# Two fused transformer layers: layer 1's feed-forward in steps beside its attention, layer 0's experts packed into fewer rounds

## The chip, the cores and the metric

The kernel runs on one core of one Trainium2 chip. The metric is the device time of one execution, in microseconds. The kernel before takes 2185.24 us (median of 3 runs, 2185.12 to 2186.42).

## The reference, cut to what matters

```
x: (8, 512, 256), so 4096 tokens of 256 numbers, all float32
xn = layernorm(x)
x  = x + attention0(xn) + experts(xn)           # layer 0
xn = layernorm(x)
x  = x + attention1(xn) + feed_forward(xn)      # layer 1

attention0:   16 heads of 16, softmax(q k') v, no mask, no output projection
experts:      8 experts; each token goes to the one with the largest x @ centroids';
              layernorm, relu(h w1' + b1) w2' + b2, 256 -> 1024 -> 256,
              mixed in with alpha = sigmoid(affinity)
attention1:   causal attention, then a convolution of width 3 over its output makes new
              queries, then a second causal attention with the same k and v, then out_w
feed_forward: P = x @ U1 (256 -> 64);  H = gelu(P @ V1 + b1) (64 -> 1024, tanh form);
              (H @ U2) (1024 -> 64) @ V2 (64 -> 256) + b2
```

## The kernel before, in words

The 4096 tokens are 32 tiles of 128 rows, 4 tiles to each of 8 batch items b. The sum x stays in SBUF (tile X, float32) through both layers. Each engine (PE, DVE, ACT, POOL, SP) runs one object whose `program` method walks the same lists of steps and issues only what belongs to that engine. So the order on every engine is written out by hand, by generators ("lanes") that are merged: `weave` spreads the steps of each lane evenly over one round, `interleave` takes one step of every lane in turn, or every second or third.

Attention is cut into units: one batch item and 8 of the 16 heads. Layer 0 has 16 units (numbers 0 to 15). Layer 1 has 32 (16 to 47): 16 of the first causal attention (kind 1), 16 of the second (kind 2), in the order 1.0, 1.1, 2.0, 1.2, 2.1, and so on, two units each. In the round of unit i run: `expp` of unit i (scores transposed on PE, L825, with a mask product L829 if causal; exp on ACT, L1625; the product with v on PE, L842), `maxp` of unit i+1 (scores on PE, L804; row maxima on DVE, L1199 or, causal, L1193; they are split into three bfloat16 rows and sent by DMA), and the projection of unit i+2 (`pre0`, `pre1`). A projection to q and k goes PE, L765 or the convolution L1017; ACT, L1603 (high part); DVE, L1151 (rest); POOL, L1839 and L1841 (middle and low part); then 6 DMAs from SP (`fan`), after which `maxp` may start.

Layer 0's expert feed-forward is a lane beside rounds 1 to 14: 39 tiles of up to 128 tokens of one expert, in two passes over halves of the hidden width, since only half the weights fit in SBUF. Pass `first` runs in rounds 1 to 7, 34 steps a round; in round 8 the weights of the second half are loaded (16 DMAs of 512 KB from ACT's queue, L1588 and L1590) and no expert step runs; pass `second` runs in rounds 9 to 14. Each tile's result goes to a DRAM buffer `ysd`.

Then comes `ffn`, a stage of its own between the layers: POOL gathers each token's row from `ysd` (L1911), DVE adds it to X with alpha (L1431) and computes the layer norm (L1071, L1139, with the square root's iteration on POOL, L1784 to L1790); PE transposes (L724, method `near`) and multiplies by U1 (L948); method `far` multiplies by V1 in 3 bfloat16 products (L965) into one of 3 PSUM banks, ACT computes the gelu (L1711, one instruction on 128x512), PE multiplies by U2 (L979), and `tail` by V2 (L992), which DVE adds to X (L1492). POOL adds the biases to X (L1944). All 8 items pass through this, about two at a time. The last items have the projections of units 16 and 17 beside them. ACT loads another function table before the first gelu and the exp table again after the last.

In layer 1 the maxima rotate over three PSUM banks, the projections and transposes share one bank (Ma), and the transposes of the attention's output have another (Mb). `fin1` transposes the second attention's output (L724, L1751) and multiplies it by out_w (L1043).

## Time and profile before

| | |
|---|---|
| median of 3 runs | 2185.24 us |
| profiled execution, its own time | 2184.84 us |
| its span, first to last instruction | 2183.0 us |
| PE busy | 1844.7 us, 85% |
| DVE busy | 1256.3 us, 58% |
| ACT busy | 1019.4 us, 47% |
| POOL busy | 363.4 us, 17% |
| mean granted TensorE clock | 0.934 of full |

A round begins with the first exp of its unit. By these starts, layer 0's unit 1 begins at 208.9 us, unit 2 at 284.1, unit 8 at 607.7, unit 9 at 650.0, unit 14 at 942.3, unit 15 at 986.6 (its attention ends at 1011); unit 16, the first of layer 1, begins at 1225.0. From 1345.4 on the rounds repeat in periods of four units (two of kind 2, two of kind 1). The table and the rows below are to be read with these borders. A PE that is busy in the profile may still have gaps between short matmuls, since the ends of matmuls are modelled.

### The profile page before, as it was taken

To read this page: it belongs to the slowest core of one execution; us is meant where nothing else is said; L and a number is where in the kernel's file an instruction comes from. 1 tells how busy PE (TensorE), PEld (TensorE's weight loads), DVE (VectorE), ACT (ScalarE), POOL (GpSimd) and SP (SyncE) were. 2 spreads that over 40 slices of the span, in tenths; PEclk is the share of its full clock that TensorE was granted. 3 is DMA by queue.
4 is the path that set the end of the run, shared out by engine and by line. 5 is a ranking of instruction groups with operands and counts; after the bars stand their busy time and mean duration, and the time that the engine had idled before them with its cause. 6 is when DMAs were issued, how large, how long until landed. Compare 5 with 4: busy or idle time off the path is not lost.

```text
span 2183.0 us, 31789 instructions
## 1 busy us (share of the span) xinstructions
PE 1844.7 (85%) x10767; PEld 904.5 (41%) x10777; DVE 1256.3 (58%) x3777; ACT 1019.4 (47%) x2048; POOL 363.4 (17%) x555
## 2 busy tenths in 40 slices
PE   3575799999979999994689788989898989989877
PEld 2341355554424444541234343444444444444434
DVE  4554455555554454553552775667575757666653
ACT  0232455655645555563354254445454545444444
POOL 2215211111101121213442100010010101000000
PEclk8557899999999999997799899999999999999999
DMA  7245343334374444413104245255553535452550
GB/s 144 68 141 140 67 83 71 80 72 81 64 203 57 71 62 71 61 28 92 32 20 73 38 57 74 41 75 68 69 74 56 74 53 67 65 78 41 66 59 21
DMA packets 145968, 155.87 MB, mean 71 GB/s; under 512 B 26008, under 2 KB 132784, under 8 KB 145808
## 3 DMA queue, kind: packets, MB, share of 16 engines
q1 hardware_dynamic: 123872, 114.75, 34.0%
q0 software_dynamic: 10048, 14.44, 3.7%
q10 hardware_dynamic: 11888, 24.64, 3.5%
q8 instruction: 88, 1.44, 0.3%
q14 instruction: 72, 0.59, 0.1%
HBM read 55.95 MB, written 33.72 MB: 41 GB/s over the span
## 4 chain that ended last, share of the span: by engine, by line
PE 60%; DVE 15%; DMA 6%; issue 6%; ACT 5%; POOL 4%; SPq 4%; DVEq 0%; ACTq 0%; POOLq 0%
PE p_PV L842 11%; PE p_S L804 8%; PE p_S L825 7%; DVE p_S L1193 5%; PE p_Ma L1017 4%; PE p_Ma L765 4%; SPq L1981 4%; PE p_Mb L896 4%; PE p_S L919 4%; DMA t_R<-ks 3%; PE p_Ma L773 2%; DVE t_rr L1151 2%; ACT t_spl L1603 2%; ACT t_R L1625 2%; POOL idd L1873 1%
## 5 line engine op out<-in xcount | busy, mean ns | idle before, releaser
L1625 ACT ACTIVATE t_R<-p_S 128x512 f32<-128x512 f32 (+1 forms) x1216 | 669.2, 576 | 469.4 <-PE p_S L829 312.1
L1193 DVE CUSTOM_DVE_ANT_0 p_S<-p_S,t_NM 128x128 f32<-128x128 f32 (+3 forms) x1024 | 473.1, 522 | 141.7 <-PE p_S L804 138.8
L804 PE MATMUL p_S<-t_R 96*128 96x512 bf16 (+3 forms) x1536 | 454.8, 338 | 67.0 <-DMA t_R<-ks 34.2
L1199 DVE TENSOR_REDUCE t_mx<-p_S 128x1 f32<-128x512 f32 x512 | 346.2, 686 | 255.2 <-PE p_S L804 242.5
L825 PE MATMUL p_S<-t_R 99*128 99x512 bf16 (+3 forms) x1536 | 466.6, 331 | 16.8 <-ACT t_R L1625 6.5
L842 PE MATMUL p_PV<-t_R 128*17 128x512 f32 (+3 forms) x3072 | 324.1, 494 | 8.9 <-ACT t_R L1625 8.7
L804 PEld LDWEIGHTS p_S<-t_R 96*128 96x128 bf16 x1536 | 135.5, 99 | 393.3 <-issue 167.2
L1839 POOL CAST t_spl<-t_rr 128x512 bf16<-128x512 f32 x80 | 49.0, 612 | 996.7 <-DVE t_rr L1151 996.7
L825 PEld LDWEIGHTS p_S<-t_R 99*128 99x128 bf16 x1536 | 150.2, 98 | 150.8 <-ACT t_R L1625 73.2
L829 PE MATMUL p_S<-t_NM 128*128 128x128 bf16 x1024 | 195.6, 220 | 0.0
L1193 DVE DVE_READ_ACCUMULATOR2_ANT t_mx<- 128x1 f32 x1024 | 144.9, 141 | 0.0
L829 PEld LDWEIGHTS p_S<-t_NM 128*128 128x128 bf16 x1024 | 101.0, 99 | 39.3 <-issue 8.3
L896 PE MATMUL p_Mb<-t_R,t_NM 128*128 x184 | 97.0, 608 | 7.6 <-DMA t_NM<-hTd 3.1
L919 PE MATMUL p_S<-t_R,t_NM 128*128 x392 | 100.9, 379 | 0.0
L842 PEld LDWEIGHTS p_PV<-t_R 128*17 128x17 f32 x3072 | 50.9, 95 | 115.9 <-issue 87.1
L1017 PE MATMUL p_Ma<-t_NM,t_R 128*128 128x512 f32 x192 | 97.8, 664 | 0.0
L1841 POOL TENSOR_TENSOR t_spl<-t_rr,t_spl 128x512 bf16<-128x512 f32 x80 | 92.6, 1157 | 6.4
L1151 DVE SCALAR_TENSOR_TENSOR t_rr<-p_Ma,t_BQK,t_spl 128x512 f32<-128x512 f32 x48 | 36.0, 751 | 97.2 <-ACT t_spl L1603 97.2
L919 PEld LDWEIGHTS p_S<-t_R,t_NM 128*128 128x128 f32 x392 | 73.7, 190 | 17.9 <-issue 2.3
L1603 ACT ACTIVATE t_spl<-p_Ma,t_BQK 128x512 bf16<-128x512 f32 x48 | 33.0, 688 | 91.1 <-PE p_Ma L765 81.6
L1603 ACT ACTIVATE t_spl<-p_Ma,t_CB 128x512 bf16<-128x512 f32 x16 | 11.0, 687 | 131.1 <-PE p_Ma L1017 131.1
L765 PE MATMUL p_Ma<-t_R,t_WQ 128*128 128x512 f32 x128 | 63.9, 623 | 7.2 <-DVE t_rr L1151 5.8
(236 smaller groups left out, 2114.1 us busy)
## 6 DMA issues: line engine op xcount, KB each, us to landing
t_R<-t_spl SPq DMA_DIRECT2D x480, 128.0 KB
t_R<-in_w ACTq DMA_DIRECT2D x32, 512.0 KB, 8.8
t_R<-ks SPq DMA_DIRECT2D x96, 128.0 KB
ks<-t_spl SPq DMA_DIRECT2D x16, 384.0 KB, 7.4
...
```

The lines of the kernel that those rows point to most:

```text
L765: t = self.nc.tensor.matmul(M[:, :], m.WQ[:, cc, off:off + 128], xT[:, cc, :], start=(cc == 0), stop=(cc == 1))
L804: t = self.nc.tensor.matmul(bank[:, z, :], qa[0:96, h, qb * 128:(qb + 1) * 128], ka[0:96, h, 0:n], start=True, stop=True)
L825: t = self.nc.tensor.matmul(bank[:, z, :], ka[0:99, h, kb * 128:(kb + 1) * 128], qa[0:99, h, n0:512], start=True, stop=not u.causal)
L829: t = self.nc.tensor.matmul(bank[:, z, 0:128], m.identb, m.maskk, start=False, stop=True)
L842: t = self.nc.tensor.matmul(m.PV[32 * j:32 * j + 17, n0:512], vt[:, kb, 4 * g + j, :], m.P1[kb][j] if u.causal else m.P[p % 2][:, j, :], s ...
L896: z = self.nc.tensor.matmul(m.MB[i][:, :], m.hT[t % 2][:, c, :], m.W1[:, bass.ds(self.regs[t], 1), c, :], start=(c == 0), stop=(c == 1))
L919: x = self.nc.tensor.matmul(M[:, 0:256], m.AT[:, k, :], m.W2[:, bass.ds(self.regs[t], 1), k * 256:k * 256 + 256], start=(k == 0), stop=(p ...
L1017: t = self.nc.tensor.matmul(M[:, :], m.CW[:, i, c * 128:c * 128 + 128], m.cT[:, cc, k:k + 512], start=(i == 0), stop=(i == 5))
L1193: x = nc.vector.tensor_tensor_reduce(out=sc, in0=sc, in1=m.maskq[:, 512 - n:512], scale=1.0, scalar=NEG, op0=ALU.add, op1=ALU.max, accum_o ...
L1199: nc.vector.tensor_reduce(m.mx[:, g, i:i + 1], m.S1[s1_bank(k)][:, :], AX.X, ALU.max).then_inc(s.s1_read, 1)
L1625: nc.scalar.activation(m.P1X[kb][j0 // per] if u.causal else m.P[p % 2][:, j0:j0 + per, :], m.s2_bank(k)[:, 0:per * n].rearrange("p (j n) ...
L1841: g.tensor_tensor(m.spl[:, z, 2, :], m.rr[:, :], m.spl[:, z, 1, :], ALU.subtract).then_inc(s.lo_done, 1)
```

## The change

The `ffn` stage as a stage is gone. Layer 0 and layer 1 are one loop of 48 rounds.

- Experts: `first` takes 40 steps in each of rounds 1 to 5 and its last 35 in round 6. The load of the second half of the weights is in round 6 behind them. `second` takes 24 steps in round 7 behind a pause, 35 in each of rounds 8 to 11 and the rest in round 12. Rounds 13, 14 and 15 have no expert steps.
- Gathers and norms of layer 1 (`arrive(b)`): items 0 and 1 in rounds 13 and 14, the others in every fourth round from 18. The add of the gathered row and the normalisation move from DVE to POOL (L1718, L1720, L1732); DVE keeps the statistics. Layer 1's weights are requested by SP at round 14, the rest at round 17. Unit 16's and 17's projections are in rounds 14 and 15.
- The feed-forward of item b (`forward(b)`), 19 steps, is spread over four rounds of layer 1 each (item 0 over rounds 15 to 17): U1, split, eight times `wide` and `bend`, then `narrow` (U2 for all eight blocks at once, from a buffer G of 8 x 512 numbers a partition).
- gelu(h) is no longer one ACT instruction. `wide`: ACT adds the bias into G (L1529) and squares into W with the scale sqrt(0.044715) (L1533); POOL adds 1 (L1749) and multiplies by h (L1751). `bend`: ACT tanh (L1547); POOL adds 1 (L1756) and multiplies by h (L1758). The factor 0.5 is applied where `narrow`'s result is copied (L1556). There is one buffer W, so one block is under way at a time.
- V2's product is accumulated into the same PSUM bank as out_w's, in `final(b)`, and DVE adds both to X in one instruction for each half.
- The maxima rotate over two PSUM banks in both layers; every other use in both layers rotates over three (Ma, Mb, S1[2]).
- The second attention's convolution, and with it its k from DRAM, comes earlier in its round: after the third of the 9 steps of its lane (`pre`), where it came at the 13th turn of a lane that ran every second turn. SP issues the loads of q and k in one step.

```diff
-    for i in range(16):
+    forward = [e.forward(b) for b in range(NB)]
+    for i in range(48):
+        b, r = (i - 10) // 4, (i - 10) % 4
+        if i == 14:
+            e.load_layer1()
+        if i == 17:
+            e.load_late()
         lanes = [e.expp(u[i])]
-        if i < 15:
+        if i < 47:
             lanes.append(e.maxp(u[i + 1]))
-        if i < 14:
-            lanes.append(e.pre0(u[i + 2]))
+        if i == 14:
+            lanes.append(chain(e.near(0), steps(1), e.pre(u[16])))
+        elif i == 15:
+            lanes.append(chain(e.pre(u[17]), take(forward[0], 2), e.near(1)))
+        elif i < 46:
+            lanes.append(e.pre(u[i + 2]))
...
-        if 1 <= i < 8:
-            lanes.append(take(first, 34 if i < 7 else 60))
-        if i == 8:
-            lanes.append(e.weights(1))
-        if 9 <= i < 15:
-            lanes.append(take(second, 34 if i < 14 else 60))
+        if 1 <= i < 6:
+            lanes.append(take(first, 40))
+        if i == 6:
+            lanes.append(chain(take(first, 60), e.weights(1), steps(10)))
+        if i == 7:
+            lanes.append(chain(steps(12), take(second, 24)))
+        if 8 <= i < 13:
+            lanes.append(take(second, 35 if i < 12 else 60))
+        if i == 13:
+            lanes.append(e.arrive(0))
+        if i == 14:
+            lanes += [e.arrive(1), e.causal_masks()]
...
+        if i in (16, 17):
+            lanes.append(take(forward[0], 9 if i == 16 else 20))
...
+        if i >= 18:
+            if r == 0 and b < NB:
+                lanes.append(e.arrive(b))
+            if r == 1 and b < NB:
+                lanes.append(chain(steps(2), e.near(b), steps(4)))
+            if i < 46:
+                lanes.append(take(forward[(i - 14) // 4], 5 if (i - 14) % 4 < 3 else 20))
+        if i and u[i - 1].kind == 2 and u[i - 1].c:
+            lanes.append(chain(steps(6), e.final(u[i - 1].b), steps(2)))
         weave(e, *lanes)
```

On ACT:

```diff
+    def wide(self, b, f, i):
+
+        e, m, s, k = self.e, self.m, self.s, 8 * b + f
+        e.wait_ge(s.h_mm, k + 1)
+        e.wait_ge(s.q_mm, b)
+        self.nc.scalar.activation(m.G[:, f, :], m.MB[i][:, :], ACT.Identity,
+                                  bias=m.FBI[:, f:f + 1]).then_inc(s.h_done, 1)
+        e.wait_ge(s.h_done, k + 1)
+        e.wait_ge(s.h_gelu, k)
+        self.nc.scalar.activation(m.W, m.G[:, f, :], ACT.Square, scale=GELU_A ** 0.5).then_inc(s.h_sq, 1)
...
+    def bend(self, b, f):
+        e, m, s, k = self.e, self.m, self.s, 8 * b + f
+        e.wait_ge(s.h_arg, k + 1)
+        self.nc.scalar.activation(m.W, m.W, ACT.Tanh, scale=GELU_C).then_inc(s.h_tanh, 1)
```

On POOL (`bend` there is the same with h_tanh, and writes G):

```diff
+    def wide(self, b, f, i):
+        e, m, s, k = self.e, self.m, self.s, 8 * b + f
+        if f == 0:
+            self.base1(b)
+        e.wait_ge(s.h_sq, k + 1)
+        a = self.mark(self.nc.gpsimd.tensor_scalar(m.W, m.W, 1.0, None, ALU.add))
+        e.wait_ge(s.g_own, a)
+        self.nc.gpsimd.tensor_tensor(m.W, m.W, m.G[:, f, :], ALU.mult).then_inc(s.h_arg, 1)
```

On PE, `wide` and the wait of `maxp` for its PSUM bank:

```diff
+    def wide(self, b, f, i):
+        e, m, s = self.e, self.m, self.s
+        M = self.mbank(i, s.h_done, 8 * b + f + 1)
...
+        for z, (vv, pp) in enumerate(((m.VA, 0), (m.VA, 1), (m.VB, 2))):
+            t = self.nc.tensor.matmul(M[:, :], vv[:, f * 128:(f + 1) * 128], m.PT[:, pp, :],
+                                      start=(z == 0), stop=(z == 2))
+        t.then_inc(s.h_mm, 1)
...
-                if k >= LAYER1 + 3:
-                    e.wait_ge(s.s1_read, k - 2)
-                elif k >= 2:
-                    e.wait_ge(s.s1_read, min(k - 1, LAYER1))
+                if k >= 2:
+                    e.wait_ge(s.s1_read, k - 1)
```

The order of the instructions shows where these steps land. ACT's queue at the load of the second weights (t_R<-in_w; ACTIVATE t_R<-p_S is an exp). Before, in round 8, the first rows:

```order
L1588 DMA t_R<-in_w 128x2x512
L1625 ACTIVATE t_R<-p_S 128x512
L1590 DMA t_R<-in_w 128x1024
L1603 ACTIVATE t_spl<-p_S,t_BQK 128x512
L1625 ACTIVATE t_R<-p_S 128x512
L1588 DMA t_R<-in_w 128x2x512
```

Of the changed kernel, in round 6, behind the last expert tile's copy (L1609):

```order
L1609 COPY t_NM<-p_Mb 128x256
L1444 DMA t_R<-in_w 128x2x512
L1446 DMA t_R<-in_w 128x1024
L1444 DMA t_R<-in_w 128x2x512
L1446 DMA t_R<-in_w 128x1024
L1478 ACTIVATE t_R<-p_S 128x512
L1444 DMA t_R<-in_w 128x2x512
```

The 16 loads have 8 exps among them where they had 29 exps and 2 other instructions.

PE's queue in a round of kind 1, around the convolution for a unit of kind 2 (MATMUL p_Ma<-t_NM,t_R x6). L810 and L903 are the transposes of the maxima that end the first half of `maxp`. Before:

```order
L810 MATMUL p_S<-t_ident,t_mx 16x128
L825 MATMUL p_S<-t_R 128x128
L829 MATMUL p_S<-t_NM 128x128
...
L842 MATMUL p_PV<-t_R 17x256 x4
L804 MATMUL p_S<-t_R 128x128 x4
L1017 MATMUL p_Ma<-t_NM,t_R 128x512 x6
```

Of the changed kernel (p_S<-t_ident,t_R is a transpose of the first attention's output; t_AF holds U1; p_Mb<-t_ident,t_O is the transpose of the output of the unit before):

```order
L751 MATMUL p_S<-t_ident,t_R 128x128 x4
L918 MATMUL p_S<-t_R 128x512
...
L897 MATMUL p_S<-t_R 128x256 x2
L822 MATMUL p_Ma<-t_R,t_AF 128x512 x2
L897 MATMUL p_S<-t_R 128x256 x2
L950 MATMUL p_Mb<-t_ident,t_O 128x128 x4
...
L918 MATMUL p_S<-t_R 128x512
L922 MATMUL p_S<-t_R,t_B1T 128x128
L806 MATMUL p_Ma<-t_NM,t_R 128x512 x6
```

The convolution stands before the transpose of the first half of the maxima, by 25 rows (L806 at row 3526, L903 at 3551 of PE's queue), where it stood behind it by 11 (L810 at 4420, L1017 at 4431).

ACT's queue in layer 1, where a unit of kind 1 is projected (t_spl<-p_Ma,t_BQK). Before:

```order
L1625 ACTIVATE t_R<-p_S 128x512 x4
L1603 ACTIVATE t_spl<-p_Ma,t_BQK 128x512
L1625 ACTIVATE t_R<-p_S 128x512
L1636 COPY t_O<-p_PV 128x512
L1603 ACTIVATE t_spl<-p_Ma,t_BQK 128x512
L1625 ACTIVATE t_R<-p_S 128x512 x2
L1625 ACTIVATE t_R<-p_S 128x384 x4
```

Of the changed kernel (L1529 is the bias add into G, L1533 the square, L1547 the tanh):

```order
L1464 ACTIVATE t_spl<-p_Ma,t_BQK 128x512
L1478 ACTIVATE t_R<-p_S 128x512
L1529 ACTIVATE t_R<-p_Mb,t_GB 128x512
L1533 ACTIVATE t_R<-t_R 128x512
L1490 COPY t_O<-p_PV 128x512
L1464 ACTIVATE t_spl<-p_S,t_BQK 128x512
L1478 ACTIVATE t_R<-p_S 128x512 x2
L1547 ACTIVATE t_R<-t_R 128x512
L1478 ACTIVATE t_R<-p_S 128x384 x4
L1478 ACTIVATE t_R<-p_S 128x512
L1529 ACTIVATE t_R<-p_S,t_GB 128x512
L1533 ACTIVATE t_R<-t_R 128x512
```

Between square and tanh, and between tanh and the next square, stand 2 to 6 other instructions. ACT's queue has one ACT_TABLE_LOAD in the changed kernel, at its start, and three before.

## Rows read from the trace of the kernel before

**Rows 1.** The page: busy time of each engine, then 40 slices.
```profile
PE 1844.7 (85%) x10767; PEld 904.5 (41%) x10777; DVE 1256.3 (58%) x3777; ACT 1019.4 (47%) x2048; POOL 363.4 (17%) x555
PE   3575799999979999994689788989898989989877
```

**Rows 2.** Busy by stretch: from:to, length, each engine (count), clock, DMA share, GB/s.
```profile
208.90:284.10 75.20, 51.91 (x240) 26.32 (x241) 32.69 (x64) 30.65 (x69) 24.00 (x26) 0.82 0.28 55
284.10:607.70 323.60, 316.52 (x1567) 163.09 (x1565) 187.90 (x357) 191.80 (x433) 59.06 (x66) 1.00 0.38 75
607.70:650.00 42.30, 34.24 (x154) 10.32 (x154) 26.48 (x50) 19.61 (x35) 4.98 (x6) 0.92 0.84 223
650.00:942.30 292.30, 279.24 (x1309) 142.71 (x1310) 141.09 (x248) 161.53 (x374) 53.68 (x63) 0.98 0.42 67
942.30:986.60 44.30, 43.59 (x215) 21.15 (x213) 25.08 (x45) 27.99 (x65) 6.03 (x8) 1.00 0.17 25
986.60:1011.00 24.40, 19.05 (x103) 3.53 (x103) 3.35 (x9) 17.38 (x33) 2.12 (x3) 1.00 0.05 7
1011.00:1225.00 214.00, 143.21 (x557) 60.94 (x568) 110.79 (x301) 71.92 (x111) 80.42 (x152) 0.84 0.24 54
1464.80:1584.20 119.40, 106.27 (x790) 52.60 (x786) 80.29 (x314) 56.26 (x107) 10.61 (x12) 0.99 0.49 66
```

**Rows 3.** PE's waits from 1011 to 1225: us in total, times, longest.
```profile
PE p_Ma L724 <- DVE t_NM L1139: 32.6, 3, 22.5
PE p_S L965 <- DVE t_R L1482: 15.7, 5, 5.7
```

**Rows 4.** Timeline of PE at 1120 to 1135: start, us, what.
```profile
1120.57 1.88 PE L948 MATMUL p_Ma<-t_R 128*128 128x512 f32 x4
1124.04 1.47 PE L965 MATMUL p_S<-t_R 128*128 128x512 bf16 x6
1125.44 1.08 PE L979 MATMUL p_S<-t_R 128*64 128x512 f32 x4
1131.79 1.03 PE L992 MATMUL p_Mb<-t_R 128*128 128x256 f32 x4
1132.65 0.60 PE L724 MATMUL p_Ma<-t_ident,t_NM 128*128 128x128 f32 x4
```

**Rows 5.** PE's waits from 607.7 to 655.
```profile
PE p_S L765 <- DMA t_R<-in_w: 4.6, 1, 4.6
PE p_S L765 <- DMA t_xTb<-xTd: 3.4, 1, 3.4
```

**Rows 6.** PE's waits from 1464.8 to 1584.2, one period of layer 1.
```profile
PE p_S L804 <- DMA t_R<-ks: 3.2, 1, 3.2
PE p_Mb L856 <- ACT t_O L1636: 2.3, 5, 0.7
PE p_Ma L724 <- DVE t_rr L1151: 1.6, 1, 1.6
PE p_Ma L773 <- DVE t_rr L1151: 0.9, 2, 0.5
PE p_Ma L765 <- DVE t_rr L1151: 0.8, 2, 0.4
```

**Rows 7.** Groups by line: busy us, mean ns, idle before. First three 1011 to 1225.
```profile
L1711 ACT ACTIVATE t_R<-p_S,t_R 128x512 f32<-128x512 f32 x64 | 43.5, 687 | 50.6 <-PE p_S L965 40.5 <-remote 7.9 <-PE p_PV L979 1.1
L1693 ACT COPY t_R<-p_Ma 128x512 f32<-128x512 f32 x16 | 9.4, 586 | 40.6 <-PE p_Ma L724 40.6
L1625 ACT ACT_TABLE_LOAD x1 | 1.3, 1283 | 6.5 <-POOL t_X L1944 6.5
L1841 POOL TENSOR_TENSOR t_spl<-t_rr,t_spl 128x512 bf16<-128x512 f32 x6 | 6.9, 1158 | 0.5
L1839 POOL CAST t_spl<-t_rr 128x512 bf16<-128x512 f32 x6 | 3.7, 611 | 108.2 <-DVE t_rr L1151 108.2
```

**Rows 8.** Durations of one line: ns min/median/max, first and last start.
```profile
L1841 POOL TENSOR_TENSOR t_spl<-t_rr,t_spl x80: 1149/1157/1162, 31.2 to 2104.2; 128x512 bf16<-128x512 f32 x80
L1856 POOL TENSOR_TENSOR t_X<-t_X,t_on x32: 719/724/1052, 180.9 to 1012.3; 128x256 f32<-128x256 f32 x32
```

More of the change, by code:

```diff
@@ L568, in add_norm, with pre @@
     def add_norm(self, b, k): pass
-    def pre0(self, u):
-        if u.c == 0:
+    def pre(self, u):
+        if u.kind == 2:
+            if u.c == 0:
+                if u.b in (0, NB - 1):
+                    yield from steps(5)
+                for cc in range(2):
+                    self.turn_c(u.b, cc, self.bank())
+                    yield
+            self.convolve(u, self.bank())
+            yield
+            yield from steps(6)
+            return
+        if u.kind == 0 and u.c == 0:
             self.load_x(u.b)
@@ L1620, in scores @@
         elif u.causal:
[L1621 to L1622 removed]
+            e.wait_ge(s.pv_mm, 128 if kb else 127)
         elif p >= 2:
@@ L1704, in far @@
-    def far(self, b):
-        nc, e, m, s = self.nc, self.e, self.m, self.s
-        for f in range(8):
-            k = 8 * b + f
-            e.wait_ge(s.v1_mm, k + 1)
-            if k >= 4:
-                e.wait_ge(s.u2_mm, k - 3)
-            nc.scalar.activation(m.HT[k % 4], m.hb[k % 3][:, :], ACT.Gelu_apprx_tanh,
-                                 bias=m.FBI[:, f:f + 1]).then_inc(s.gelu, 1)
-            yield
-    def tail(self, b):
-        e, m, s = self.e, self.m, self.s
-        e.wait_ge(s.u2_mm, 8 * b + 8)
-        if b >= 2:
-            e.wait_ge(s.y2_mm, 2 * b - 2)
-        self.nc.scalar.copy(m.QS[b % 2], m.qb[b % 2][:, :]).then_inc(s.qs_done, 1)
-        yield from steps(4)
```

966 lines of the change are left out of this document (405 added, 561 removed).

## The prediction

> **What bounds the kernel now.** I read the page first: PE is busy 85% of the span, DVE 58%, ACT 47%, POOL 17% [rows 1]. So PE bounds, and the question is where its 338 idle us lie. I cut the span at the borders of the rounds [rows 2]. In rounds 2 to 7 (expert steps beside attention) PE is busy 316.5 of 323.6 us, in rounds 9 to 13 279.2 of 292.3. Round 8, without expert steps, has 34.2 of 42.3. The stage between the layers takes 214 us, with PE busy 143.2, at a mean clock of 0.84. A period of layer 1 (4 units) takes 119.4 us, with PE busy 106.3, DVE 80.3, ACT 56.3 and POOL 10.6. PE's waits in the stage are a start (32.6 us in 3 waits for normalised rows) and a hand-over from DVE (15.7) [rows 3]. Waits in a period are small and many: k from DRAM 3.2 us, the rest of the split (t_rr) 1.6 + 0.9 + 0.8, the output's copy 2.3 [rows 6].
>
> No matmul goes away. The change takes PE work of a stage that PE fills to two thirds and puts it where PE is filled to 89%. So the gain is the idle time that vanishes, less the waits that the steps bring with them.
>
> **Layer 0, rounds 1 to 15.** PE is busy 51.9 + 316.5 + 34.2 + 279.2 + 43.6 = 725.5 us in rounds 1 to 14 [rows 2]. Rounds 13 and 14 now hold attention only. What such a round takes I read from round 8: 42.3 us, less 3.4 us of waiting for x [rows 5], less about 3.4 us for its half clock. The last is worked out from the mean clock 0.92: 8% of 42.3 us lost against full clock is 3.4 us. That leaves 35.5 us, of which PE works 34.2 - 3.4 = 31. Rounds 1 to 12 keep the rest of the work: 725.5 less 6.8 for the clock of rounds 8 and 9, less 31 for round 13, less 26 for round 14 (it had no projection, about 5) = 662. Their idle time: 23.3 in round 1 (routing, unchanged), 11 rounds at 1.3 = 14 (rounds 2 to 7 show 7.1 for six), and for the weights 3. Sum 702, so round 12 ends at 208.9 + 702 = 911.
>
> On the weights: before, PE waits 4.6 us for them after a whole round of spaced loads [rows 5]. Now the 16 loads stand within a quarter of round 6 (the order: 8 exps among them), some 14 us. 8.4 MB at the 223 GB/s of round 8 [rows 2] take 38 us, at the rate of a quiet moment less. The first expert step that needs them is a third into round 7, about 16 us in. Loads begin some 23 us before round 6 ends, so they have 39 us: just enough. I take 3 us, bounds 0 and 15.
>
> Round 13: 35.5 us. Round 14: 37, with the first transposes. Round 15: it took 24.4 without maxima and projection; now it has both, U1 and two transposes: 40. SP issues 12 loads of layer 1 at the head of round 14, ahead of that round's maxima and its fans of 6; POOL's gathers stand before its split of q and k. For both I add 3 us, bounds 0 and 25 (the longest wait of rows 3 is 22.5). Layer 1 then starts at 911 + 35.5 + 37 + 40 + 3 = 1026, not at 1225.
>
> **Layer 1, a period.** PE's steps for one batch item, from their rows [rows 4]: V1 24 products at 1.47 - 0.17 per 6 (the tail of one overlaps the next) = 5.2; U2 four pairs at about 0.95 = 3.8; U1 1.7; transposes 2 x 0.55 = 1.1; V2 1.7. Sum 13.5 us, and all of it is on the path, since PE is the bound.
>
> What goes: the convolution stands some 25 rows before the middle of the maxima instead of 11 behind, so k and q start about 5 us earlier and the 3.2 us for k go. Three rotating banks replace the one shared bank (Ma), so of 3.3 us of waits for t_rr I drop 2.8. The clock's 1% is 1. Sum 7.0 [rows 6, 2]. Late next behind k is the copy of O (2.3), which stays.
>
> What comes: ACT gets, per block of the gelu, a bias add of 0.69 (as L1711), a square and a tanh of about 0.59 (as L1693) [rows 7], 1.87 us for 0.69: 15.0 us per item, and 3.5 for four copies and a scaled copy. 56.3 + 18.5 = 75 of 130 us: not the bound. But ACT's queue is in order: in `wide` two instructions, 1.28 us, stand before the next exp, and only two banks lie between PE's scores and the exps. PE meanwhile has its own 0.65 us of V1 and the maxima. I take 0.25 us of stall for each of 16 steps = 4. The bounds are 0 and the whole burst, 8 x (1.28 + 0.59) = 15.
>
> POOL per block: two adds and two products on 128x512. The nearest rows are a one-input cast, 611 ns, and a two-input op, 1157 ns [rows 7]: 3.5 us a block, 28 an item; with joins, normalisation, the split and the base add (together about 18, an estimate from L1856, L1839 and L1841) POOL works 57 of 130 us. A step of `forward` comes every 5.4 us or so (5 in a round of 27), and POOL's pair takes 1.8, so the tanh seldom waits. Two banks for the maxima instead of three: DVE needs 0.7 to 0.9 us for a single maximum, PE sends one each 1.1 us on the average; only bursts wait. This was never seen in layer 1; bounds 0 and 2 a period, I take 0. DVE loses two adds of V2 an item and the gathers' adds, and keeps statistics; at 80 of 130 us that costs nothing.
>
> So a period goes from 119.4 by +13.5 - 7.0 + 4.0 = +10.5. Layer 1's eight items: 8 x 10.5 = 84. From 1225.0 to 2183.0 it took 958.0; now 1042. The two table loads (the gelu's, and the exp's again, 1283 ns) go with the stage [rows 7].
>
> **Sum.** 1026 + 1042 = 2068 of span. The profiled execution was 1.84 us longer than its span, and the median of the runs 0.4 above it: 2070 us, 115 less than 2185 (5.3%).
>
> **A rule that speaks against it.** L1841, the nearest to POOL's new products, took 1149 to 1162 ns in all 80 cases, with DVE at work beside it; L1856, with two float32 inputs, took 724 and once 1052 [rows 8]. The Trainium skill (GPSIMD Engine Reference, Specifications) says that POOL shares its SBUF interfaces with VectorE and contends with it when a DVE instruction runs in a two-port mode or has two SBUF inputs. By the 80 cases nothing is added. By the rule, DVE's new neighbours could stretch POOL's pair; it is the second half of the slower rival below. The skill's ScalarE: Activation LUTs (Table sets) lists tanh in the exp set; no run so far shows a tanh. The built order has no table load in layer 1, and the sum goes by that.
>
> **The rivals.**
> *PE is filled.* The new steps slip into the gaps. A period cannot be under 106.3 + 13.5 = 119.8; with 3 idle it is 122.8, +3.4. Layer 1 takes 958 + 8 x 3.4 = 985; rounds 13 to 15 take PE's own 32 each, so it starts at 911 + 96 = 1007: 1992, as a time 1994. For it: rounds 2 to 7 are filled to 98%. Against it: these steps hang on four engines, expert steps on two.
> *ACT's bursts block the exps.* Two thirds of the full burst: +10 instead of +4, and 48 more in all: 2118; with poor banks for the maxima, 2130. For it: two score banks. Against it: ACT is busy less than half of a period [rows 2], so it catches up.
> *The start stays.* Gathers, norms and weights are still chains: the waits of 32.6 [rows 3] come back in rounds 13 to 15, which also run light on PE and at half clock in part: 2105.
> *The relay is on the path (slower).* For each of the 64 blocks ACT must wait twice for POOL in its own queue, at the tanh and at the next square. If POOL's pair (1.8 us) were exposed each time, 128 x 1.8 = 230 us: 2300. It decides from 115 / 128 = 0.9 us of exposure per hand-over. Contention like the one case of 1052 ns against 724 would make the pair 2.6, which 2 exps between do not cover and 5 do. For it: one W, two engines in order, POOL also with gathers and 12 small steps of the square root between a square and its sum. Against it: the spacing of 5.4 us.
> *It does nothing.* If layer 0 were bound by something else than PE, moving experts would not shorten it, but the stage of 214 us goes in any case.
>
> **Chances.** Forecast 57% (own range 2045 to 2100), PE filled 13%, bursts 15%, start stays 9%, relay slower 4% and 2% at no change. Range to hold 8 in 10: 2015 to 2128, which takes in most of the bursts, all of the start, and the upper part of "PE filled". Faster by over 0.2% (what a measurement of this kernel can tell) 93%, within 0.2% 2%, slower 5%.
>
> **What will show it.** The first causal exp at about 1026; rounds 13, 14, 15 at 35 to 40 us; a period near 130 with PE busy about 120; no wait for the second weights over 5 us; k's wait gone from PE's waits in layer 1; ACT about 75 and POOL about 57 us busy a period; L1749 and L1756 about 0.6 us, L1751 and L1758 about 1.16. I am wrong if the period is over 137 or under 125, if layer 1 starts after 1045, or if ACT's waits for POOL at L1547 and L1533 sum to over 30 us.

## The result, and the profile after

The changed kernel takes 2229.76 us (median of 4 runs, 2224.86 to 2234.62) against 2185.62 in the same session. The ratio is 1.0202, 95% interval [1.0179, 1.0224]: 44 us slower, where 115 faster was forecast. The profiled execution's span is 2232.8 us.

Its page answers to [rows 1]:

```profile
PE 1884.2 (84%) x10777; PEld 910.8 (41%) x10777; DVE 1211.5 (54%) x3653; ACT 1096.7 (49%) x2178; POOL 824.9 (37%) x935
...
PE   3573899999799999988778888888888898888877
```

PE's share is what it was (84% against 85%). The weak slices in the middle (the 4 and 6 of [rows 1], the stage) are gone; in their place the 9s of layer 1 have turned into 8s. The work was moved as planned, but PE is idle as large a share of the time as before.

The stretches, to be held against [rows 2] (from:to, length, busy of PE, PEld, DVE, ACT, POOL with counts, clock, DMA share, GB/s). They are round 1; rounds 2 to 6; 7; 8 to 12; 13; 14; 15; and one period of layer 1:

```profile
215.20:290.80 75.60, 61.21 (x276) 31.02 (x277) 33.39 (x65) 33.19 (x75) 17.88 (x20) 0.86 0.29 62
290.80:589.80 299.00, 288.53 (x1390) 150.55 (x1388) 159.74 (x306) 169.42 (x388) 53.08 (x59) 0.98 0.42 96
589.80:648.20 58.40, 49.51 (x227) 22.70 (x228) 28.13 (x51) 30.47 (x69) 8.63 (x10) 0.97 0.44 82
648.20:946.30 298.10, 284.66 (x1323) 145.23 (x1321) 139.96 (x244) 163.51 (x376) 54.38 (x65) 0.98 0.41 63
946.30:988.20 41.90, 33.98 (x157) 9.95 (x158) 29.04 (x61) 19.44 (x36) 26.31 (x43) 0.92 0.36 59
988.20:1033.10 44.90, 38.14 (x165) 11.26 (x164) 30.14 (x61) 20.31 (x38) 22.16 (x40) 0.85 0.60 114
1033.10:1073.20 40.10, 33.04 (x167) 11.20 (x166) 23.71 (x84) 24.95 (x44) 13.00 (x12) 0.91 0.37 50
1376.30:1519.60 143.30, 123.80 (x849) 59.69 (x846) 85.28 (x326) 73.85 (x136) 76.20 (x75) 0.95 0.42 58
```

Round 12 ends at 946.3 (forecast 911). Rounds 13 to 15 take 41.9, 44.9 and 40.1 (forecast 35.5, 37, 40, and 3). Layer 1 starts at 1073.2 (forecast 1026): 152 us earlier than before, 47 later than forecast. From there it takes 1159.6 us (958 before, forecast 1042): 118 more than forecast. A period has 123.8 us of PE in 143.3 us, where 120 in 130 was forecast.

PE's waits in that period, to be held against [rows 6] (total us, times, longest), and ACT's one long wait for POOL:

```profile
PE p_S L918 <- ACT t_R L1478: 6.7, 6, 4.6
PE p_S L897 <- DVE t_mx L1125: 4.3, 9, 0.7
PE p_S L903 <- DVE t_mx L1125: 4.1, 8, 0.5
PE p_Ma L950 <- ACT t_O L1490: 2.1, 2, 1.6
PE p_Mb L950 <- ACT t_O L1490: 1.9, 2, 1.0
```
```profile
ACT t_R L1522 <- POOL t_R L1742: 4.6, 1, 4.6
```

The wait for k from DRAM (3.2 in [rows 6]) and those for t_rr are gone from this period, as forecast. Three came or grew: one of 4.6 us for an exp; 8.4 for the row maxima, which have two banks now; and more at the output's copy (4.0 against 2.3). For the maxima PE waited 2.5 us in the period of before:

```profile
PE p_S L810 <- DVE t_mx L1193: 1.5, 3, 0.5
PE p_S L804 <- DVE t_mx L1193: 1.0, 4, 0.3
```

L1522 is ACT's copy of the high part of P = x U1 to a second place, which PE's next product reads. The timeline shows how one copy holds PE (start, us, what; idle before in brackets):

```profile
1453.46 0.69 ACT L1464 ACTIVATE t_spl<-p_Ma,t_CB 128x512 bf16<-128x512 f32 x1 [4.61 <-PE p_Ma L806]
...
1454.99 0.61 POOL L1681 CAST t_spl<-t_rr 128x512 bf16<-128x512 f32 x1 [20.80 <-DVE t_rr L1088]
...
1455.68 1.15 POOL L1683 TENSOR_TENSOR t_spl<-t_rr,t_spl 128x512 bf16<-128x512 f32 x1
...
1456.78 0.61 POOL L1740 CAST t_R<-t_R 128x512 bf16<-128x512 f32 x1
1457.47 1.15 POOL L1742 TENSOR_TENSOR t_R<-t_R 128x512 bf16<-128x512 f32 x1
...
1458.71 0.61 ACT L1522 COPY t_R<-t_R 64x512 bf16<-64x512 bf16 x1 [4.57 <-POOL t_R L1742]
...
1459.35 0.87 ACT L1478 ACTIVATE t_R<-p_S 128x384 f32<-128x384 f32 x2
...
1459.89 0.50 PE L918 MATMUL p_S<-t_R 99*128 99x384 bf16 x1 [4.56 <-ACT t_R L1478]
```

POOL waits for DVE's rest of the convolution, splits that (L1681, L1683), and only then splits P (L1740, L1742). ACT's copy waits for it, the exps wait behind the copy, and PE waits for an exp (L918 <- L1478, 4.6 us). The copy's duration was in the forecast (one of "four copies"), its wait was not.

The gelu's operations in the same period, to be held against [rows 7] (busy us, mean ns, idle before them):

```profile
L1749 POOL TENSOR_SCALAR t_R<-t_R 128x512 f32<-128x512 f32 x8 | 11.9, 1490 | 14.6 <-ACT t_R L1533 14.6
...
L1751 POOL TENSOR_TENSOR t_R<-t_R 128x512 f32<-128x512 f32 x8 | 10.2, 1270 | 0.7
...
L1547 ACT ACTIVATE t_R<-t_R 128x512 f32<-128x512 f32 x8 | 5.1, 633 | 0.8 <-POOL t_R L1751 0.8
```

POOL's add takes 1.49 us, not 0.61, and the pair 2.76, not 1.8. POOL is busy 76 us a period, not 57. Yet ACT waits only 0.8 us for it in the tanhs of a period: the relay is hidden there. In the whole run ACT waits for POOL 15.8 us at L1547 and 7.2 at L1533, 23.0 together, and 29.1 us in 7 waits at the copy L1522.

### The profile page after: what moved, and what is told of

The parts are those of the page before. It is cut to its first block, busy times and chain, and to the rows that moved or that the text cites. A ratio compares the mean times of both kernels' runs of the same rounds, so it can differ in the third digit from the quotient of the medians.

```text
span 2232.8 us, 32221 instructions
## 1 busy us (share of the span) xinstructions
PE 1884.2 (84%) x10777; PEld 910.8 (41%) x10777; DVE 1211.5 (54%) x3653; ACT 1096.7 (49%) x2178; POOL 824.9 (37%) x935
## 4 chain that ended last, share of the span: by engine, by line
PE 63%; DVE 10%; ACT 7%; POOL 7%; issue 6%; DMA 4%; SPq 3%; ACTq 0%; DVEq 0%; POOLq 0%
PE p_PV L937 11%; PE p_S L897 9%; PE p_S L918 8%; PE p_Mb L990 3%; PE p_S L1013 3%; DVE p_S L1125 3%; SPq L1884 3%; ACT t_R L1478 3%; PE p_Ma L870 2%; PE p_S L922 2%; PE p_S L870 2%; DMA t_NM<-hTd 2%; PE p_Mb L870 1%; PE p_Ma L806 1%; PE p_Mb L806 1%
## 5 line engine op out<-in xcount | busy, mean ns | idle before, releaser
L1478 ACT ACTIVATE t_R<-p_S 128x512 f32<-128x512 f32 (+1 forms) x1216 | 676.8, 575 | 489.3 <-PE p_S L922 269.8
L1125 DVE CUSTOM_DVE_ANT_0 p_S<-p_S,t_R 128x128 f32<-128x128 f32 (+3 forms) x1024 | 478.5, 515 | 295.0 <-PE p_S L897 294.7
L918 PE MATMUL p_S<-t_R 99*128 99x512 bf16 (+3 forms) x1536 | 485.5, 341 | 65.7 <-ACT t_R L1478 64.5
L897 PE MATMUL p_S<-t_R 96*128 96x512 bf16 (+3 forms) x1536 | 465.9, 344 | 83.2 <-DVE t_mx L1125 38.5
L937 PE MATMUL p_PV<-t_R 128*17 128x512 f32 (+3 forms) x3072 | 338.6, 514 | 4.2 <-ACT t_R L1478 2.8
L918 PEld LDWEIGHTS p_S<-t_R 99*128 99x128 bf16 x1536 | 154.2, 100 | 218.5 <-ACT t_R L1478 112.9
L1681 POOL CAST t_spl<-t_rr 128x512 bf16<-128x512 f32 x80 | 49.0, 613 | 436.9 <-DVE t_rr L1088 436.9
L922 PE MATMUL p_S<-t_R,t_B1T 128*128 128x128 bf16 x1024 | 204.7, 225 | 0.0
L1749 POOL TENSOR_SCALAR t_R<-t_R 128x512 f32<-128x512 f32 x64 | 95.3, 1489 | 125.0 <-ACT t_R L1533 124.9
L922 PEld LDWEIGHTS p_S<-t_R,t_B1T 128*128 128x128 bf16 x1024 | 103.8, 101 | 47.8 <-issue 15.5
L1756 POOL TENSOR_SCALAR t_R<-t_R 128x512 f32<-128x512 f32 x64 | 95.3, 1489 | 64.7 <-ACT t_R L1547 64.7
L1837 POOL DMA_DIRECT2D ysd<-t_NM x39 | 34.1, 874 | 227.9 <-ACT t_NM L1609 227.9
L1683 POOL TENSOR_TENSOR t_spl<-t_rr,t_spl 128x512 bf16<-128x512 f32 x80 | 92.5, 1157 | 6.5
L1826 POOL DMA_INDIRECT t_NM<-h0d,t_gidx x39 | 37.8, 970 | 148.7 <-PE p_S L975 51.1
L1751 POOL TENSOR_TENSOR t_R<-t_R 128x512 f32<-128x512 f32 x64 | 81.2, 1269 | 5.4
L1758 POOL TENSOR_TENSOR t_R<-t_R 128x512 f32<-128x512 f32 x64 | 81.1, 1267 | 5.3
```

What stands on the lines that cost most here:

```text
L897: t = self.nc.tensor.matmul(bank[:, z, :], qa[0:96, h, qb * 128:(qb + 1) * 128], ka[0:96, h, 0:n], start=True, stop=True)
L918: t = self.nc.tensor.matmul(bank[:, z, :], ka[0:99, h, kb * 128:(kb + 1) * 128], qa[0:99, h, n0:512], start=True, stop=not u.causal)
L922: t = self.nc.tensor.matmul(bank[:, z, 0:128], m.identb, m.maskk, start=False, stop=True)
L937: t = self.nc.tensor.matmul(m.PV[32 * j:32 * j + 17, n0:512], vt[:, kb, 4 * g + j, :], m.P1[kb][j] if u.causal else m.P[p % 2][:, j, :], s ...
L1125: x = nc.vector.tensor_tensor_reduce(out=sc, in0=sc, in1=m.maskq[:, 512 - n:512], scale=1.0, scalar=NEG, op0=ALU.add, op1=ALU.max, accum_o ...
L1478: nc.scalar.activation(m.P1X[kb][j0 // per] if u.causal else m.P[p % 2][:, j0:j0 + per, :], m.s2_bank(k)[:, 0:per * n].rearrange("p (j n) ...
```

## The experiments

All times are medians of runs, and each ratio is to the kernel before, run beside it on the same chip; a round's length is that between the first exps of two units. Each run is set against the one that it differs from by its edit; these two were not always run side by side, and the kernel before had medians of 2182.5 to 2185.6 us in the five sessions. So a difference of 2 or 3 us says nothing.

### The copy of P's high part one step later, in the changed kernel

```diff
         self.split(b)
         yield
+        self.dup(b)          # ACT's copy L1522, with its wait for POOL; ACT's split(b) is empty
+        yield
         for f in range(8):
```

> The changed kernel (2229.8 us) with one edit: ACT's copy of P's high part (L1522), which waits for POOL's split, gets a step of its own, one step (about 5 us) later. Theory 1 (this copy stands in ACT's queue before exps that PE needs): its wait of 4.6 us a period, after which PE shows a wait of 4.6 us for an exp, goes in all 8 items: 2230 - 8 x 4.6 = 2193, and PE's wait for L1478 in a period falls from 6.7 to about 2. Rival (something else is late just then, the wait only moves): 2225 to 2235.

2165.15 us, ratio 0.9916 [0.9897, 0.9935]: 65 us less, more than either theory gave. A period is 134.3 us or 131.8, in turn, and this is what is left of PE's waits in one of the longer (1367.3 to 1501.6):

```profile
PE p_S L900 <- DVE t_mx L1128: 4.9, 10, 1.0
PE p_S L906 <- DVE t_mx L1128: 4.1, 8, 0.5
PE p_Ma L953 <- ACT t_O L1493: 1.8, 1, 1.8
PE p_Mb L953 <- ACT t_O L1493: 1.2, 2, 1.0
PE p_S L921 <- ACT t_R L1481: 0.7, 3, 0.2
```

The layer starts at 1073.6, as in the changed kernel, so all of it is layer 1's: 1159.6 to 1095.5. The theory had counted the one wait, 8 x 4.6. Of the 9.0 us that this period loses, 6.0 are the waits for exps, and 2.9 is PE's own busy time (123.8 to 120.9, the mean clock of a period from 0.95 to 0.97). The round with the copy falls from 44.7 to 37.0. The edit also moves every later step of the item by one; that part wasn't run by itself, but the two waits that the theory named, ACT's for POOL and PE's behind it, are gone.

### The gelu's chain left out

The square and tanh on ACT and the four operations of POOL are left out for every block, so the feed-forward has no gelu. On ACT (POOL's `wide` and `bend` go likewise):

```diff
-        self.nc.scalar.activation(m.W, m.G[:, f, :], ACT.Square, scale=GELU_A ** 0.5).then_inc(s.h_sq, 1)
...
-        self.nc.scalar.activation(m.W, m.W, ACT.Tanh, scale=GELU_C).then_inc(s.h_tanh, 1)
```

> The changed kernel without gelu: h + b1 is used as it is; left out are ACT's square and tanh (128 instructions) and POOL's 256 adds and products. It prices all of the chain at once: ACT's bursts, the hand-overs to POOL, POOL's load. Theory 1 (the chain is what made a period 143.3 us and not 130): a period of 130 to 133, time 2140 to 2155. Rival (PE's own steps, the clock and the two banks of the maxima make it): 1 or 2 us a period, time 2212 to 2222.

2179.44 us (10 runs), ratio 0.9982 [0.9964, 0.9999]: 50 us less, between the two. The period goes from 143.3 to 138.0. The round with the copy still takes 44.7 us, and the 4.6 us wait stands though POOL is busy 32 us a period, not 76. So that wait was never POOL's load; by the timeline above it is the order of its queue. Rounds 16 and 17 fall from 40.4 and 43.6 to 29.9 and 33.9.

### Three banks for layer 1's maxima, in the changed kernel

The main lines (the first two cut at their end; the waits of PE and the reads of DVE follow them):

```diff
-                bank = m.S1[k % 2][:, 0:len(js) * n]
+                bank = m.S1[s1_bank(k)][:, 0:len(js) * n]   # 3 banks from unit 16's maxima on
...
-        return self.banks % 3
+        return self.banks % (2 if self.two else 3)             # the other uses rotate over 2
```

> The changed kernel with layer 1's maxima on three PSUM banks again and all other uses from round 14 on rotating over two (Ma, Mb). Theory 1 (two banks for the maxima cost PE 5.9 us a period: its waits for L1125 at L897 and L903 were 2.5 us in the period before and are 8.4 after): 4 to 6 us a period less, time 2182 to 2198. Rival (with two banks for the rest, projections, blocks of the feed-forward and the output's transposes now wait for one another): between 2220 and 2250.

2197.34 us, ratio 1.006 [1.0038, 1.0081]: 32 us less, as expected. The waits for maxima of a period fall from 8.4 to 4.9 us; it takes 139.1 in place of 143.3.

### Two banks in the kernel before

```diff
-    return k % 2 if k < LAYER1 else (k - LAYER1 + 1) % 3
+    return k % 2 if k < LAYER1 else (k - LAYER1 + 1) % 2
...
-                if k >= LAYER1 + 3:
-                    e.wait_ge(s.s1_read, k - 2)
+                if k >= LAYER1 + 2:
+                    e.wait_ge(s.s1_read, k - 1)
```

> The kernel before with only the maxima of layer 1 on two PSUM banks instead of three. Theory 1 (the third bank is worth about 4 us a period of four units, as three banks gave the changed kernel back 33 us): 2205 to 2220. Rival (in the order of before PE sends maxima at an even pace, so two banks do): 2183 to 2192.

2217.39 us, ratio 1.0146 [1.0116, 1.0176]: 35 us more, as expected. One period (1471 to 1594), first three of PE's waits:

```profile
PE p_S L804 <- DVE t_mx L1193: 6.1, 15, 0.8
PE p_S L804 <- DMA t_R<-ks: 1.9, 1, 1.9
PE p_Ma L724 <- DVE t_rr L1151: 1.6, 1, 1.6
```

None of the 15 waits is over 0.8 us; PE's waits for maxima before had been 2.5 us in all. The period goes from 119.4 to 123.0.

### POOL's pairs as one instruction each on DVE, in the changed kernel

```diff
-        a = self.mark(self.nc.gpsimd.tensor_scalar(m.W, m.W, 1.0, None, ALU.add))
-        e.wait_ge(s.g_own, a)
-        self.nc.gpsimd.tensor_tensor(m.W, m.W, m.G[:, f, :], ALU.mult).then_inc(s.h_arg, 1)
+        self.nc.vector.scalar_tensor_tensor(out=m.W, in0=m.W, scalar=1.0, in1=m.G[:, f, :],
+                                            op0=ALU.add, op1=ALU.mult).then_inc(s.h_arg, 1)
```

`bend` is changed in the same way, and POOL's four operations are gone.

> The changed kernel with gelu's add and product as one instruction on DVE (two for each block, about 0.75 us each) in place of four on POOL (5.5 us a block). POOL falls from about 76 to 32 us busy a period, DVE rises from 85 to 97. Theory 1 (POOL's long pair of 2.8 us is on the path): 3 to 6 us a period less, time 2180 to 2205. Rival (ACT's waits for POOL were only 0.8 us a period outside the copy of P, and DVE's queue gets longer): no gain, 2225 to 2245.

2301.29 us, ratio 1.0531 [1.0498, 1.0564]: 71 us more; both theories missed. PE's first two waits of one period (1377.2 to 1533.8), a wait of DVE, and the new instruction's group:

```profile
PE p_S L903 <- DVE t_mx L1125: 8.4, 8, 2.3
PE p_S L897 <- DVE t_mx L1125: 7.5, 13, 2.2
```
```profile
DVE t_R L1217 <- ACT t_R L1545: 14.4, 7, 4.2
```
```profile
L1217 DVE SCALAR_TENSOR_TENSOR t_R<-t_R 128x512 f32<-128x512 f32 x8 | 5.8, 725 | 15.8 <-ACT t_R L1545 14.4 <-issue 1.4
```

The pair costs 0.73 us here against POOL's 2.76, and the kernel is slower all the same: DVE stands 14.4 us a period at L1217 waiting for ACT's square, the maxima queue behind it, and PE's waits for maxima go from 8.4 to 15.9. The period goes from 143.3 to 156.6, of which 6.1 us are PE's busy time at a lower mean clock (0.91 in place of 0.95). DVE is also 10 us a period busier; no run separates that from the waiting. A short instruction that waits for a slow partner was dear in a queue that PE hangs on.

### The experts' packing alone, in the kernel before

```diff
-        if 1 <= i < 8:
-            lanes.append(take(first, 34 if i < 7 else 60))
-        if i == 8:
-            lanes.append(e.weights(1))
-        if 9 <= i < 15:
-            lanes.append(take(second, 34 if i < 14 else 60))
+        if 1 <= i < 6:
+            lanes.append(take(first, 40))
+        if i == 6:
+            lanes.append(chain(take(first, 60), e.weights(1), steps(10)))
+        if i == 7:
+            lanes.append(chain(steps(12), take(second, 24)))
+        if 8 <= i < 13:
+            lanes.append(take(second, 35 if i < 12 else 60))
```

> The kernel before with only the experts' steps moved as in the change (40 a round, the second weights in round 6, the end in round 12); the stage of the feed-forward stays. Theory 1 (packing costs by itself, since rounds 13 and 14 run on attention alone and rounds 6 to 11 are crowded: the changed kernel ended round 12 at 946, not at 911): layer 0's attention ends at about 1035 to 1045 instead of 1011, time 2205 to 2220. Rival (the working of the prediction: PE's work is only moved, so it ends at 911 + 35.5 + 31 + 24.4 = 1002): 2173 to 2180.

2215.24 us, ratio 1.0143 [1.0124, 1.0162]: 33 us more, as expected. Stretches: rounds 2 to 5; 6 and 7; 8 to 12; 13 and 14:

```profile
289.80:521.90 232.10, 227.51 (x1122) 121.57 (x1120) 129.30 (x248) 136.47 (x314) 44.99 (x51) 1.00 0.38 78
521.90:646.00 124.10, 111.23 (x498) 52.37 (x497) 58.80 (x108) 63.87 (x142) 16.51 (x19) 0.92 0.49 124
646.00:940.20 294.20, 282.74 (x1322) 145.12 (x1321) 140.80 (x244) 163.04 (x376) 54.38 (x65) 0.99 0.41 64
940.20:1012.80 72.60, 61.59 (x283) 14.90 (x281) 51.30 (x96) 37.92 (x67) 7.17 (x9) 0.93 0.20 25
```

Round 12 ends at 940.2 without any of layer 1's new work, near the changed kernel's 946.3. Rounds 13 and 14 take 72.6; the forecast had 35.5 + 37 = 72.5 for them. So an attention round was priced right, and rounds 1 to 12 were not. PE's two longest waits, in total, in rounds 6 and 7:

```profile
PE p_S L827 <- ACT t_R L1627: 5.7, 5, 1.5
PE p_S L898 <- DMA t_NM<-hTd: 4.5, 1, 4.5
```

### The packing with the weights in a round of their own, in the kernel before

```diff
         if i == 6:
-            lanes.append(chain(take(first, 60), e.weights(1), steps(10)))
+            lanes.append(take(first, 60))
         if i == 7:
-            lanes.append(chain(steps(12), take(second, 24)))
+            lanes.append(e.weights(1))
         if 8 <= i < 13:
-            lanes.append(take(second, 35 if i < 12 else 60))
+            lanes.append(take(second, 40 if i < 12 else 80))
```

> The kernel before, with its experts packed into rounds 1 to 12 as in the run of the packing alone (that took 2215.2 us, unit 13 at 940.2, unit 15 at 1012.8), but the second half's weights are loaded in round 7, spread over the whole of it and without expert steps, and the second pass takes 40 steps in each of rounds 8 to 11 and the rest in round 12. Theory (the 16 loads in a quarter of round 6 hold up ACT's queue, and round 7 starts late on its expert steps: rounds 6 and 7 took 124.1 us together): rounds 6 and 7 take 55 + 42 = 97, rounds 8 to 11 some 64 each, unit 13 begins at about 928, the time is 2200 to 2207. Rival (the density of expert steps beside attention costs, wherever the loads stand): unit 13 at 938 or later, 2212 to 2225.

2203.12 us, ratio 1.0083 [1.0067, 1.01]: 12 us less than the packing as it was, as expected. Rounds 6 and 7, and 8 to 12:

```profile
521.90:617.90 96.00, 85.54 (x425) 38.03 (x423) 58.16 (x108) 53.75 (x113) 12.86 (x15) 0.99 0.63 149
617.90:930.50 312.60, 303.25 (x1396) 157.03 (x1396) 141.16 (x245) 175.53 (x405) 57.74 (x68) 0.99 0.42 63
```

Together 408.6 us against 418.3 above: PE is busy 5 us less (its clock in rounds 6 and 7 is 0.99, not 0.92) and idle 4 to 5 less. The edit also takes the 24 expert steps out of round 7, so this is the worth of the loads and those steps together. The packing still costs 19 us after that. The loads are also later now, and PE waits for the last of them at the end of round 7:

```profile
PE p_S L827 <- DMA t_R<-in_w: 4.2, 1, 4.2
```

### The convolution earlier in its lane, alone, in the kernel before

```diff
-LATE2 = 4
+def late2(b):                  # and late2(u.b) wherever LATE2 stood
+    return 4 if b in (0, NB - 1) else 0
```

> The kernel before with only the convolution of items 1 to 6 four turns of its lane earlier (items 0 and 7 as they were, since their input is not there sooner). Theory 1 (PE's wait for k from DRAM, 34.2 us in 8 waits, goes for six of them, some 20 us, as it went in the changed kernel): 2160 to 2170. Rival (the wait is replaced by one for the output's copy or for the split): 2180 to 2190.

2139.62 us, ratio 0.9795 [0.9778, 0.9812]: 43 us less, faster than both expectations. A lane's pause of 4 turns ahead of the convolution is dropped for items 1 to 6, as the change has it in its own lanes. Rounds 27.4, 27.3, 30.3 and 27.1 make 112.1 us for 119.4. The theory had counted k's wait alone, and that went as it said (34.2 to 14.9 us in the whole run). But PE's wait at L724 for the rest of the split went as well (9.4 us in all), and in each period PE is busy 103.7 us in place of 106.3, at a mean clock of 1.00 in place of 0.99. PE's longest wait total in a period (1453 to 1565.1) is now:

```profile
PE p_S L813 <- DVE t_mx L1196: 2.0, 4, 0.5
```

### Copy and banks together; then the spaced weights; then no chain

The first has both edits in the changed kernel, the second also the spaced weights (the diff above), the third the first's two edits with the gelu's chain left out.

> The changed kernel with both edits that helped: the copy of P's high part one step later, and three banks for layer 1's maxima with two for the rest. Theory 1 (two separate waits of PE, 65 us and 33 us): 2125 to 2140. Rival (both filled the same gap, or with two banks for the rest the later copy collides): 2150 to 2170.

> The changed kernel with the copy of P's high part in a step of its own and three banks for layer 1's maxima (that took 2147.9 us), and the second weights loaded over the whole of round 7, the second pass in rounds 8 to 12 at 40 steps and the rest. If the crowded loads cost what rounds 6 and 7 suggest: 2133 to 2140. If the density costs: 2145 to 2158. Layer 1's period is not touched (130 to 131).

> The changed kernel with the copy of P's high part in a step of its own and three banks for layer 1's maxima (2147.9 us), and of the gelu only the bias add is left: ACT's square and tanh and POOL's two adds and two products for each of the 64 blocks are left out, so its output is not the feed-forward of the reference. Theory (the chain of ACT and POOL still costs, by ACT's bursts ahead of an exp and POOL's work ahead of the split of q and k): the period falls from 130.6 to 123 to 125, rounds 16 and 17 by 6 us each, 2090 to 2105 in all. Rival (with the copy away and the third bank the chain is hidden): the period stays over 128, 2130 to 2145.

Copy and banks: 2147.93 us, ratio 0.9846 [0.9821, 0.987], 17 below the copy alone: just under the rival's 2150, and above the theory's 2140. With the spaced weights: 2135.93 us, ratio 0.9772 [0.9753, 0.979], 12 less again, as expected. Without the chain: 2102.59 us, ratio 0.9619 [0.9589, 0.9649], 45 less, as expected in total but not in its parts. One period and rounds 16 and 17, of copy and banks:

```profile
1355.30:1486.50 131.20, 118.97 (x849) 59.00 (x847) 85.72 (x326) 73.62 (x136) 76.30 (x75) 0.99 0.46 64
1068.20:1105.80 37.60, 29.65 (x207) 13.63 (x204) 22.00 (x80) 21.13 (x39) 25.66 (x21) 0.95 0.40 54
1105.80:1153.10 47.30, 35.67 (x224) 16.07 (x222) 21.69 (x79) 21.58 (x39) 34.81 (x29) 0.89 0.38 65
```

and without the chain:

```profile
1331.20:1458.80 127.60, 116.56 (x848) 58.39 (x846) 84.05 (x326) 64.43 (x119) 32.33 (x43) 1.00 0.46 66
1069.30:1099.90 30.60, 27.28 (x205) 12.98 (x203) 21.80 (x80) 16.65 (x30) 4.28 (x5) 1.00 0.49 67
1099.90:1133.60 33.70, 30.80 (x225) 14.46 (x223) 20.93 (x79) 17.15 (x31) 12.15 (x12) 1.00 0.54 91
```

The next period of copy and banks takes 130.6. So in the steady period the chain costs 3.6 us (6 to 8 expected), in rounds 16 and 17 alone 20.6 (12 expected). There item 0's feed-forward runs at 9 steps a round in place of 5.

### The first item's feed-forward spread over three rounds

```diff
         if i in (16, 17):
-            lanes.append(take(forward[0], 9 if i == 16 else 20))
+            lanes.append(take(forward[0], 6))
...
-            if i < 46:
-                lanes.append(take(forward[(i - 14) // 4], 5 if (i - 14) % 4 < 3 else 20))
+            if i == 18:
+                lanes.append(chain(take(forward[0], 20), take(forward[1], 2)))
+            elif i < 46:
+                n = 6 if i < 21 else 5
+                lanes.append(take(forward[(i - 14) // 4], n if (i - 14) % 4 < 3 else 20))
```

> The changed kernel with the copy in a step of its own, three banks and the spaced weights (2135.9 us), and the first item's feed-forward spread further: 6 steps in each of rounds 16, 17 and 18 and the second item's in 2, 6, 6 and the last 6 of rounds 18 to 21, where rounds 16 and 17 had 9 each. Theory (in rounds 16 and 17 four blocks of the gelu come in 37 to 47 us, and ACT waits 16 us there for POOL at the tanh and the next square, with PE behind it; a block's chain is 0.69 + 0.59 + 2.8 + 0.59 + 2.8 = 7.5 us, which 9 steps a round do not give it): rounds 16 and 17 take 34 and 37 in place of 37.4 and 47.3, round 18 stays near 34, the time is 2120 to 2127. Rival (rounds 16 and 17 are long by POOL's work beside the chain: the joins, norms and bias adds of the next item, which stay): 2131 to 2140.

2142.76 us, ratio 0.9813 [0.9797, 0.9829]. Both expectations missed: there is no gain on 2135.93, and the ratio is above that run's 0.9772 [0.9753, 0.979], some 7 us slower by the medians. Rounds 16 and 17 did fall, from 84.7 to 66.2 us. Round 18 took back 13.5 of these (46.8 for 33.3) and rounds 19 to 21 4.4. Rounds 16 to 21 take 217.7 us here and 218.3 there. The two profiled executions took 2139.1 and 2141.1 us, so where the medians' 7 us lie the traces can't show. The end of the item shows what came in round 18 (start, us, what):

```profile
1151.86 1.51 POOL L1776 TENSOR_SCALAR t_R<-t_R 128x512 f32<-128x512 f32 x1
1153.46 1.26 POOL L1778 TENSOR_TENSOR t_R<-t_R 128x512 f32<-128x512 f32 x1
1154.86 6.54 PE L858 MATMUL p_Ma<-t_R 128*64 128x512 f32 x16 [3.48 <-POOL t_R L1778]
```

U2's product reads all eight blocks at once. PE waits 3.5 us for POOL's last product and then runs its 16 matmuls at half clock (0.50 in the profile from 1154 to 1160). That these two make up the whole of what round 18 lost wasn't tested.

## Why the prediction was wrong, step by step

Of the three signs of being wrong that the prediction named, two came: the period is 143.3 us (137 was the limit), and layer 1 starts at 1073.2 (1045). The third, ACT's waits for POOL at L1547 and L1533, sums to 23.0 us and stays under its 30.

Forecast and result are 160 us apart. The spans split it into 47 before layer 1 starts and 118 in it, less 5 for roundings and the time around the span (2070 was forecast for 2068 of span; 2229.8 is the median, the profiled span 2232.8).

**"Rounds 1 to 12 keep the rest of the work ... 662 ... Sum 702."** Failed. The PE time was carried over from the rounds of before and a stall was priced for the weights alone (3 us); round 12 ended 35 us late. The packing alone brings 29 of these (940.2 against 911); the other 6 are not assigned. Ten of the 29 are the 16 loads among 8 exps, with the expert steps of round 7 (the spaced run's 930.5). In the changed kernel and in the packed one PE shows no wait for the weights themselves. It waited for ACT, in whose queue the loads stand between the exps: in the packed run 5.7 us for exps in rounds 6 and 7 (1.1 in the spaced one), and 4.5 us for an expert tile's hidden rows. That the loads cause the first is read from the order of the queue, and the spaced run, which changes two things, agrees; it has a wait of 4.2 us for the weights instead. The other 19 are spread: in the spaced run rounds 2 to 14 have PE busy 679 us of 715, in the kernel before 674 of 703 [rows 2]. That is about 6 us more PE time for the same products and 7 more idle, and round 1 ends 5 us later. Such numbers are good to a few us only: the three kernels that don't pack the experts begin round 2 at 279.1, 280.2 and 284.1 with the same code up to there. Which step of a crowded round loses the 19 stayed open.

**"Round 13: 35.5 us. Round 14: 37 ... Round 15: 40", plus 3.** The first two are right without the new work (72.6 measured in the packed run for 72.5). With the gathers and norms the first two take 86.8, at a clock of 0.92 and 0.85, round 15 its 40.1: 11 too few in all. The bounds of 0 and 25 held this; the value taken was too low.

**"Two banks for the maxima instead of three ... I take 0", bounds 0 and 2.** Failed. The third bank is worth 32 us in the changed kernel and 35 in the kernel before, 4.2 us a period in the one (143.3 to 139.1) and 3.6 in the other (119.4 to 123.0), both above the bound of 2. I compared DVE's mean rate with PE's, and fifteen waits of 0.4 us on the average add up. The prediction said itself that "only bursts wait", and put their cost at nothing without a row.

**"In `wide` two instructions stand before the next exp ... I take 0.25 us of stall for each of 16 steps = 4."** Near for the steady state, where the chain as a whole costs 5.3 us a period in the changed kernel and 3.6 with the copy and the banks mended. But here is the largest failed step: a wait was put at nothing. I went through `wide` and `bend` for what they put into ACT's queue and counted the copies behind `split` among "four copies", by their durations. One of them waits for POOL, and POOL has the convolution's split ahead; moving that copy one step later gave 64 us of layer 1. The prediction asked that question of the tanh and the square, 128 hand-overs that wait 23.0 us in the whole run, and not of the 8 copies, which wait 29.1 with PE behind them.

**"What goes ... 7.0."** Right as a sum, and partly by luck in its parts. The prediction gave 4.2 of it to the convolution (k's wait and the clock) and 2.8 to the rotating banks. The early convolution gives 7.3 a period by itself: about 3.2 for k, 1.6 of the waits for t_rr, and 2.6 of PE's busy time. With the copy and the banks mended the period is 130.6 to 131.2, against 129.9 forecast, and its other terms are near (PE is busy 14 to 15 us more than in the run of the convolution, 13.5 forecast; the chain costs 3.6, 4.0 forecast). But that kernel has the third bank and the later copy, which the forecast thought it could do without. So the period was right for a kernel that this one wasn't.

**Rounds 16 and 17** were priced as any others. They take 84.0 us, about 20 more than two rounds of the period forecast, and without the gelu's chain they take 20.6 less. Copy, banks and these are 64 + 20 + 20 = 104 of the 118; the copy's 64 is the fall in layer 1's length from 1159.6 to 1095.5, the banks' 20 the further fall to 1075.1 (alone, without the later copy, the third bank gives 37 there, so the two edits overlap in part). The remaining 14 are not assigned.

**POOL's pair "takes 1.8".** Wrong in size (2.76); ACT hardly waits for it in the steady period. The recorded 57 us of POOL's work doesn't follow from its terms either: 28 + 18 is 46, and 57 comes out only with the 10.6 of [rows 2] added, which hold the split already. Measured are 44.1 for the chain and 32.1 for the rest. The stretching by DVE's work that the prediction set against itself isn't seen: L1751 takes 1261 to 1281 ns in all 64 cases, L1758 1260 to 1277. So the 1270 against the 1157 of [rows 7] is the price of this operation on these tiles, not of single collisions. The Trainium skill (GPSIMD Engine Reference, Engine selection) calls POOL's one-input operations roughly line-rate next to DVE and its two-input ones about twice as slow. For two inputs the traces agree: 1270 ns against 691 for a float32 128x512 sum on DVE (L1474 of the kernel before). But the one-input add in float32 is the slower of POOL's two, 1490 ns against 1270, so there the measurement decides; DVE did both in one instruction of 725 ns. The tanh needed no table load of its own: the trace has a single one in the whole kernel, at its start.

None of the rivals gave this result. The relay, with a 4% chance, was the only slower one, and it was about another hand-over. What should have carried more chance is the class: any instruction in ACT's queue that waits for a third engine stops the exps behind it.

**The best versions.** The kernel before with the early convolution alone (ratio 0.9795) and the changed kernel with the late copy, three banks and spaced weights (0.9772) can't be told apart, and both beat the two kernels of this case. The second has the early convolution in it, so all the rest of the change, mended, adds nothing over it that could be measured. Of the change's parts that were timed alone in the kernel before, only the convolution gains (43 us); the packing costs 33 and the two banks 35.
